# A four-layer kernel on one core: the FFN down stages' next row pairs, turned on TensorE or on VectorE with transfers

## What is computed

```python
x = x + _L0_attn_a_ref(_layernorm(x), ...)   # linear attention in chunks of 128, 4 heads
x = x + _L0_ffn_ref(_layernorm(x), ...)      # 512 -> 1408 -> 512
x = x + _L0_attn_b_ref(_layernorm(x), ...)   # softmax attention over 1024 tokens
x = x + _L0_ffn_ref(_layernorm(x), ...)      # the same FFN again

def _L0_ffn_ref(x, wq_gate, s_gate, wq_up, s_up, wq_down, s_down):
    gate = jax.nn.silu(_qlinear(x, wq_gate, s_gate))
    up = _qlinear(x, wq_up, s_up)
    return _qlinear(gate * up, wq_down, s_down)
```

## Time and profile before

| | us |
|---|---|
| median of 3 runs | 955.8 |
| lowest and highest | 955.75, 956.13 |
| span of the profiled execution | 954.9 |
| down stage of block 1, from the last low matmul of tile 0 to its end | 442.0 to 474.85 |

### The profile page before, as it was taken

One profiled execution on the slowest core, in us unless ns is written; L12 is line 12 of the kernel. 1 busy time (PEld: TensorE's weight loads), 2 busy tenths in 40 slices (PEclk: granted clock), 3 DMA queues, 4 the chain that ended last, 5 costly groups with the idle time before them and its releaser, 6 DMA issues.

```text
span 954.9 us, 13285 instructions
## 1 busy us (share of the span) xinstructions
PE 941.6 (99%) x4744; PEld 534.5 (56%) x4744; DVE 608.9 (64%) x1128; ACT 460.8 (48%) x918; POOL 478.6 (50%) x487
## 2 busy tenths in 40 slices
PE   7999999999999999999999999999999999999998
PEld 4888988888744454444544455445455444544443
DVE  7555657849677586776855466445465676766543
ACT  4443334356577545664533455323454665456631
POOL 5433424477266676666840043304333566665575
PEclk9999999999999999999999999999999999999999
DMA  9401300024200000000000000000000000110001
GB/s 324 165 11 34 133 23 23 2 89 142 95 29 1 1 1 1 1 1 1 1 1 1 1 1 1 1 1 1 1 0 1 1 0 1 45 45 1 1 23 67
DMA packets 14738, 30.31 MB, mean 32 GB/s; under 512 B 2064, under 2 KB 2128, under 8 KB 14672
## 3 DMA queue, kind: packets, MB, share of 16 engines
q1 hardware_dynamic: 14672, 29.45, 8.6%
HBM read 25.22 MB, written 4.23 MB: 31 GB/s over the span
## 4 chain that ended last, share of the span: by engine, by line
PE 93%; ACT 1%; DVE 1%; POOL 1%; DMA 1%; SPq 1%; issue 0%; POOLq 0%; DVEq 0%
PE psum L2078 54%; PE psum L2325 14%; PE psum L2327 14%; PE psum L2453 7%; PE psum L2127 2%; PE psum L2464 1%; DMA bq_col<-bq 1%; PE psum L2212 1%; PE psum L2116 1%; ACT probs L1329 0%; DVE xb_lo L1983 0%; SPq L658 0%; ACT xb_hi L1335 0%; POOL wvT_lo L922 0%; POOL wo_lo L925 0%
## 5 line engine op out<-in xcount | busy, mean ns | idle before, releaser
L872 POOL TENSOR_TENSOR hid<-hid,hid_hi 128x512 f32<-128x512 f32 x88 | 102.7, 1167 | 101.6 <-DVE hid_hi L1777 101.6
L2325 PE MATMUL psum<-xf,w_gu 128*128 128x512 f16 x352 | 133.8, 380 | 0.0
L2325 PE MATMUL psum<-xf,w_s 128*128 128x512 f16 x264 | 100.0, 379 | 0.6 <-DVE up L1750 0.4
L2327 PE MATMUL psum<-xf,w_gu 128*128 128x512 f16 x264 | 100.1, 379 | 0.0
L1191 ACT ACTIVATE hid_lo<-hid 128x512 f16<-128x512 f32 x88 | 55.0, 625 | 33.0 <-POOL hid L872 33.0
L868 POOL TENSOR_TENSOR hid<-up,gate 128x512 f32<-128x512 f32 x44 | 56.0, 1273 | 23.8 <-ACT gate L1186 23.8
L2327 PE MATMUL psum<-xq,w_s 128*128 128x512 f16 x176 | 66.7, 379 | 0.0
L2325 PEld LDWEIGHTS psum<-xf,w_gu 128*128 128x128 f16 x352 | 34.3, 98 | 53.9 <-ACT acc L1176 15.5
L1186 ACT ACTIVATE gate<-gate,sg_xs 128x512 f32<-128x512 f32 x44 | 31.7, 721 | 65.7 <-DVE gate L1760 65.7
L734 POOL TENSOR_TENSOR xrstd<-xvar,minus_half 128x1 f32<-128x1 f32 x48 | 25.5, 548 | 59.2 <-DVE xvar L1448 59.2
L1777 DVE TENSOR_SCALAR hid_hi<-hid 128x512 f16<-128x512 f32 x88 | 39.1, 444 | 19.4 <-POOL hid L868 17.9
(11 more groups left out here) (308 smaller groups left out, 2560.1 us busy)
## 6 DMA issues: line engine op xcount, KB each, us to landing
cla_wide<-cla_dram SPq DMA_DIRECT2D x16, 256.0 KB, 3.3
out<-xres SPq DMA_DIRECT2D x16, 256.0 KB, 2.0
xres<-x SPq DMA_DIRECT2D x3, 1024.0 KB, 13.3
codes_gu<-gateT SPq DMA_DIRECT2D x1, 2816.0 KB, 11.5
codes_gu<-upT SPq DMA_DIRECT2D x1, 2816.0 KB, 10.7
codes_da<-downT SPq DMA_DIRECT2D x1, 1536.0 KB, 6.8
codes_db<-downT SPq DMA_DIRECT2D x1, 1280.0 KB, 11.2
xres<-x SPq DMA_DIRECT2D x4, 256.0 KB, 3.2
```

The source lines that it names most:

```text
L872: nc.gpsimd.tensor_tensor(hid[:, :], hid[:, :], hid_part(hid_hi, j, half), ALU.subtract).then_inc(rest_done, 1)
L2325: nc.tensor.matmul(bank(use[0]), w, x_operand(piece, k, False), start=start and k == 0, stop=False, skip_group_check=not start)
L2327: last = nc.tensor.matmul(bank(use[0]), w, x_operand(piece, k, True), start=False, stop=k == 1, skip_group_check=not start)
```

## The change

The twelve pairs of the down stages are no longer turned on PE. For these sets (`MOVED`):

- DVE normalises both rows of a pair into one tile of 1024 columns (`xn` or `xn_pair1`, in turns) and turns it in place in blocks of 32x32 with one instruction (`x_blocks`).
- Sixteen SBUF-to-SBUF transfers per pair (`move_blocks`) bring the blocks to their places in `turned0` or `turned1`: each takes 32 partitions, eight runs of 32 f32 (128 bytes) per partition. SP issues eight (`SP_ROWS`) and ACT the other eight (`ACT_ROWS`). Both wait for the block turn; from the third pair on also for the readers of the buffer.
- ACT, DVE and POOL read `turned` in SBUF where they read a bank or `x_first`; the `x_copy` falls away.
- `X_AFTER` becomes (2, 3, 5, 6). DVE's block turns stand ahead of tile 0 and after tiles 0, 2 and 3 (`BLOCKS_AFTER`); ACT's issues stand ahead of `y_low(0)` and after the tiles 1, 2 and 3 (`MOVE_AFTER`).
- On SP the stores of the result come after or between the moves.

```diff
-X_AFTER = (1, 3, 5, 6)
+X_AFTER = (2, 3, 5, 6)
+BLOCKS_AFTER = {0: 1, 2: 2, 3: 3}
+SQ = 32
+QUADS = P // SQ
+SP_ROWS, ACT_ROWS = (0, 1), (2, 3)
+MOVE_AFTER = {2: 2, 3: 3}
...
+    def move_blocks(queue, rows, q, i):
+        n, m = 4 * q + i, moved_n(q, i)
+        queue.wait_ge(x_blocks_done, m + 1)
+        if i < 2:
+            phase, b = {F1: ("F1", 0), B0: ("F1", 1), F3: ("F2", 0)}[q]
+            Use(queue, phase, b).read_out(delta(JT - 1, 1))
+        else:
+            queue.wait_ge(x_ab_lo, n - 1)
+            queue.wait_ge(x_t34_done, 2 * n - 2)
+            queue.wait_ge(x_2_lo_done, m - 1)
+        src = xn_pair[i % 2][:, :].rearrange("p (m c j) -> p m c j", c=QUADS, j=SQ)
+        dst = turned[i % 2][:, :].rearrange("p (m a j) -> p m a j", a=QUADS, j=SQ)
+        for a in rows:
+            for c in range(QUADS):
+                queue.dma_start(dst[c * SQ:(c + 1) * SQ, :, a, :],
+                                src[a * SQ:(a + 1) * SQ, :, c, :]).then_inc(x_moved[i % 2], 16)
...
                     extra(j)
+                if blk < 3:
+                    move_blocks(act, ACT_ROWS, NEXT_SET[blk], 0)
                 for t in range(BT):
                     u.full(down_lo(t))
...
                         i = X_AFTER.index(t)
-                        x_copy(NEXT_SET[blk], i)
...
+                    if blk < 3 and t == 1:
+                        move_blocks(act, ACT_ROWS, NEXT_SET[blk], 1)
+                    if blk < 3 and t in MOVE_AFTER:
+                        move_blocks(act, ACT_ROWS, NEXT_SET[blk], MOVE_AFTER[t])
...
+            def x_blocks(q, i):
+                m, pair = moved_n(q, i), xn_pair[i % 2]
+                if i > 1:
+                    dve.wait_ge(x_moved[i % 2], moved_all(m - 2))
+                elif i == 1:
+                    dve.wait_ge(hid1_lo_done, JT * (MOVED.index(q) + 1))
+                    dve.wait_ge(hid2_lo_done, JT * (MOVED.index(q) + 1))
+                for l in (2 * i, 2 * i + 1):
+                    dve.wait_ge(ln_rstd_done, ln_n("X", q, l) + 1)
+                    nc.vector.tensor_scalar(cols(pair, l % 2), x_row(q, l), xmv[:, 2 * l:2 * l + 1],
+                                            xrstd[:, l:l + 1], ALU.subtract, ALU.mult).then_inc(ln_xn_done, 1)
+                dve.wait_ge(ln_xn_done, ln_n("X", q, 2 * i + 1) + 1)
+                nc.vector.transpose(pair[:, :], pair[:, :]).then_inc(x_blocks_done, 1)
...
                 def x_after(t):
                     if blk < 3 and t in X_AFTER:
-                        i = X_AFTER.index(t)
-                        x_second(NEXT_SET[blk], i)
-                        if i < 3:
-                            x_normalise(NEXT_SET[blk], i + 1)
+                        x_second(NEXT_SET[blk], X_AFTER.index(t))
+                    if blk < 3 and t in BLOCKS_AFTER:
+                        x_blocks(NEXT_SET[blk], BLOCKS_AFTER[t])
...
                         down(t, down_hi(t), hid_hi, range(JT))
-                    if blk < 3 and t in X_AFTER:
-                        turn_x(NEXT_SET[blk], X_AFTER.index(t), 0)
-                        turn_x(NEXT_SET[blk], X_AFTER.index(t), 1)
```

More of the change, by code:

```diff
@@ L91 @@
 NEXT_SET = (F1, B0, F3)
+MOVED = NEXT_SET
 BLOCK_SET = (F0, F1, F2, F3)
@@ L204, in hybrid_layer_kernel @@
     X_PLACE = (0, 1, 1, 2, 3, 1)
+    xn_pair = [xn, at("xn_pair1", Z + 77824, 2 * D)]
+    turned = [at(f"turned{i}", Z + 61440 + 4096 * i, 2 * D) for i in range(2)]
     w_s = at("w_s", Z + 104448, 6 * HID, F16)
@@ L317, in hybrid_layer_kernel @@
     cla_masked = sem("cla_masked")
+    x_blocks_done = sem("x_blocks_done")
+    x_moved = [sem(f"x_moved{i}") for i in range(2)]
+    x_2_lo_done = sem("x_2_lo_done")
     cla_minus_done = sem("cla_minus_done")
@@ L471, in x_2_cols, with x_first_of @@
         return slice(0, 4 * P) if q in (B0, B1) else slice(2 * P, 4 * P)
+    def x_first_of(q, i):
+        return turned[i % 2][:, 0:D] if q in MOVED else x_first[X_PLACE[q]][:, :]
     def x_pair(t, first, i):
@@ L714, in _, with store @@
             weights(codes_db[:, :], downT[6 * P:JT * P, :], db_in)
-            for b in range(BATCHES):
-                for t in range(BT):
+            def store(b, *ts):
+                for t in ts:
                     sp.wait_ge(x_updated, updates(2 + b, t))
@@ L719, in _ @@
                     sp.dma_start(out[n * P:(n + 1) * P, :], xres[:, n * D:(n + 1) * D]).then_inc(x_out, 16)
+            for q in (F1, B0):
+                for i in range(4):
+                    move_blocks(sp, SP_ROWS, q, i)
+            move_blocks(sp, SP_ROWS, F3, 0)
+            move_blocks(sp, SP_ROWS, F3, 1)
+            store(0, 0, 1)
+            move_blocks(sp, SP_ROWS, F3, 2)
+            store(0, 2)
+            move_blocks(sp, SP_ROWS, F3, 3)
+            store(0, *range(3, BT))
+            store(1, *range(BT))
             sp.wait_ge(x_out, 4 * GT * 16)
@@ L998, in x_row_highs @@
             def x_row_highs(q, i):
+                v = X_PLACE[q]
+                if q in MOVED:
+                    m = moved_n(q, i)
+                    act.wait_ge(x_moved[m % 2], moved_all(m))
+                    if m > 1:
+                        act.wait_ge(x_2_lo_done, m - 1)
+                    first, second = turned[m % 2][:, 0:D], turned[m % 2][:, D:2 * D]
+                    nc.scalar.activation(x_2(q, i, 0), second[:, x_2_cols(q)].rearrange("p (k n) -> p k n", n=P),
+                                         ACT.Copy).then_inc(x_b2_hi, 1)
+                    nc.scalar.activation(x_ab(q, i, 0), four(first), ACT.Copy).then_inc(x_ab_hi, 1)
+                    return
                 phase, b, first, second = x_banks(q, i)
-                v = X_PLACE[q]
                 Use(act, phase, b).full(second)
@@ L1455, in x_normalise @@
                                             xrstd[:, l:l + 1], ALU.subtract, ALU.mult).then_inc(ln_xn_done, 1)
-            def x_second(q, i):
-                phase, b, first, second = x_banks(q, i)
-                n, v, t = 4 * q + i, X_PLACE[q], bank(second[0])
-                Use(dve, phase, b).read_out(first)
+            def x_blocks(q, i):
[11 more added lines that the diff above has]
+                nc.vector.transpose(pair[:, :], pair[:, :]).then_inc(x_blocks_done, 1)
+            def x_second(q, i):
+                n, v = 4 * q + i, X_PLACE[q]
+                if q in MOVED:
+                    m = moved_n(q, i)
+                    dve.wait_ge(x_moved[m % 2], moved_all(m))
+                    t, first = turned[m % 2][:, D:2 * D], turned[m % 2][:, 0:D]
+                    done = x_2_lo_done
+                else:
+                    phase, b, one, two = x_banks(q, i)
+                    Use(dve, phase, b).read_out(one)
+                    t, first, done = bank(two[0]), x_first[v][:, :], drained[two[0]]
                 dve.wait_ge(x_b2_hi, n + 1)
```

32 lines of the change are left out of this document (17 added, 15 removed).

## The result

| | kernel before | changed kernel |
|---|---|---|
| median of 4 runs each, us | 955.8 | 1036.6 |
| ratio | 1 | 1.084 (95%: 1.083 to 1.086) |
| span of the profiled execution, us | 954.9 | 1036.1 |

The direction was right and the size was not: +81 us, where +34 was forecast, and the time lies above the range (957 to 1018).

What follows compares the result with a forecast made beforehand. PE was taken as the bound: busy 99% of the span, 93% of the chain. Stage losses of +10.4 (second) and +11.6 (first and third) summed to +33.6; with 954.9 and 0.9 that gave 989.4 us, range 957 to 1018.

Steps and rivals of the forecast that it cites:

- What is removed: Down stages: 96 of 192 transposes leave PE, eight per pair for twelve pairs, 10.5 us off PE.
- The landing: Arrival of a moved pair's transfers: 2.0 us, costing nothing; at 10 us, about 5 us in the whole kernel.
- the walk: Step-by-step timing of the engines' order through the second down stage: +10.4 us there, +11.6 for the first and third.
- The price of an issue on ScalarE: ScalarE's eight transfers per pair: 0.35 us each, 2.8 for eight, 96 times in the path.
- third rival: Both queues share what an issue needs, or short runs back up: 0.53 to 0.7 us each, 1007 to 1023; chance 0.13.
- The mechanism: Down stages: ScalarE's issues delay `y_low`, so PE waits three times per stage, some 34 us in all.
- longest at tile 6: Sign in each down stage: PE's longest wait for `y_low` comes at tile 6, 6.25 us.
- The three subtractions: VectorE's subtractions for each pair in the down stages: 1.3 us for the three.
- The clock rival: PE's clock drops after the tile 6 stalls, ten matmuls costing 2.1 us more per stage: 996 us; chance 0.14.
- step 6: Stage tail: the last pair's low part on GpSimd (`x_ab_low`) ends at 485.2, adding 2.6 us.
- Free issues: Rival: ScalarE issues cost 0 to 0.1 us, VectorE's chain alone binds: 958 to 967 us; chance 0.19.
- faster: Rival: free issues, VectorE at its quickest, last low part ahead of PE, most of 10.5 kept: 945 to 953; chance 0.12.

Runs made afterwards that it cites:

- e4: Kernel before plus a probe behind its last store, groups of eight transfers in several forms and queues; SBUF-to-SBUF issues took 0.61 to 0.63 us (32 runs of 1 KB: 0.59 to 0.61).
- e2: Changed kernel, but ScalarE's eight transfers per pair became one of 128 partitions, still issued by ScalarE, rows left on their partitions; 977.3 us, ratio 1.023.
- e1: Changed kernel, but ScalarE's eight transfers per pair became one issued by SP, rows left on their partitions; 970.9 us, ratio 1.016.
- e5: Kernel before plus 32 small ScalarE transfers in each of three stages, copying a constant nobody reads; 998.2 us, ratio 1.043.
- e13: Changed kernel with the first operand of all three subtractions of a pair read from PSUM, times 0; 1026.3 us, ratio 1.074.
- e6: Changed kernel with 22, 24 and 24 unused matmuls ahead of tiles 2, 5 and 6 of the three stages; 1037.2 us, ratio 1.084.
- e14: e1 with the first operand of all three subtractions of a pair read from PSUM, times 0; 964.3 us, ratio 1.009.

## Why the prediction missed

1. **What is removed**, 10.5 us of PE: nothing speaks against it; no run tested it by itself.
2. **The block turn**, 1.2 us: 1.245. **Normalising a pair**, 1.6: 1.81 to 1.94 (single rows 0.54 to 1.49). **The landing**, 2.0: 1.9 to 2.0, and it held nobody in the changed kernel. Right, or nearly; the 0.25 us more a pair is 3 us in the walk.
3. **The price of an issue on ScalarE** is the step that failed. It was put at 0.35, "the number on which all hangs", within 0 to 0.53. It is 0.69 in a row. The 0.34 between, 96 times, is 33 us of the 47 missed. The prediction took it from SP's rows of 0.32 us, which were loads from DRAM; the stores of `out` from SBUF to DRAM, sixteen in the same trace, also took 0.33, so it is the transfers with both ends in SBUF that were dear. The row for "0.53, four times as much" was read as a price of size, and e4 and e2 show that for SBUF to SBUF size has no part in it. A flat 0.6 could be bounded by no row. The range went up to a price of 0.64 (96 x 0.29 more is 1017) and left out the 0.7 of the third rival, whose own upper end (1023) would have come within 14 us of the time.
4. **That rival's reasons** are wrong: both queues sharing what an issue needs, since one queue alone pays the same (e1, e4); short runs backing up, since 16 runs of 2 KB pay it too (e4). Its 0.7 was right by luck.
5. **The mechanism** was right in place: stalls ahead of tiles 2, 5 and 6, `y_low(4)` behind the fourth pair's issues, all three stages alike. e1 and e5, the part undone and the part alone, show it. But the sign "longest at tile 6" failed: the longest stall is ahead of tile 5. And that the one ahead of tile 6 came out at 6.2 us, forecast 6.25, is luck: tile 5 ran at the lower clock and took 7.7 us in place of 4.75, and from its start to that of tile 6 it is 13.9 us where the forecast had 11.0.
6. **The three subtractions** were priced at the kernel before's 0.41, 0.42 and 0.68, and GpSimd's sums at 0.73 and 0.91. The change moves their first operand from PSUM to SBUF, and that was in the diff. It is a term that the sum did not have: 10.3 us (e13). The kernel before shows the hold as well: in the earlier trace rows the subtraction with both operands in SBUF (L1478, `xs_lo`) took 1.75 us, and the one of the same size with one in PSUM (L1471) 0.68. The long one, from 452.27 to 454.02, began while GpSimd was busy with the operation of the row below, and ended 0.55 us behind it. The prediction took over the 1.75 and did not ask where it came from. The Trainium skill, SBUF — State Buffer, section Who interferes with whom, says that a VectorE instruction with two SBUF inputs contends with a GpSimd instruction that reads SBUF, and one with a single SBUF input does not; the traces agree (0.42 against up to 1.49 us).

```profile
451.76 1.71 POOL L907 TENSOR_TENSOR yt<-yt,sd_rows 128x512 f32<-128x512 f32 x1
```

7. **The clock rival** had chance 0.14 and +6 us. It happened, in every stage (0.78 in the stretch above), and cost nothing that e6 could give back. Its argument, that after tile 6 the loss has no stall to vanish in, overlooked that the stage's end was no longer PE's: the walk's own step 6 has GpSimd's last low part 2.6 us behind PE, more than the 2.1 in question.
8. **Free issues** and **faster** are excluded by e5 and by e14.

33.6 forecast, 33 for the issue, 3 for VectorE and 10 for the hold are 80 of the 81. The 33 and the 3 are the walk's, the 10 is measured.

## What to carry to other kernels

A transfer issued by an engine that also computes is an instruction in its order: from SBUF to SBUF each took a full 0.6 to 0.7 us here, whatever it carried, so count them and ask who waits for what is queued behind it. When an edit moves an operand from PSUM to SBUF, reprice every operation that reads it, and every GpSimd operation beside it. And before you put a price on a slower clock, ask which engine sets the end of that stretch: TensorE at 0.78 cost nothing where ScalarE and GpSimd were last.

## What the hardware showed that I had not expected

- An SBUF-to-SBUF issue took 0.61 us on SP with 256 runs, 0.61 to 0.63 on ScalarE with 16, 128 or 256 runs and with 16 or 32 KB (e4), and 0.61 with 1,024 runs and 256 KB (e2, ScalarE). In the kernel before, SP issued loads of 256 KB in 0.32 us and stores of 256 KB to DRAM in 0.33.
- VectorE's subtraction of 128 x 256 took 0.42 us with an operand in PSUM, also beside GpSimd, and up to 1.49 with both in SBUF; GpSimd's sum of the same size went from 0.73 to as much as 1.11.
- TensorE at a granted clock of 0.78 over 55 us and at 0.97 gave the same time (1036.6 and 1037.2 us).
